# Attention scores made a second time by key, with the maxima carried in rows of the stacked queries

## The reference

```python
q, k, v = (split_heads(x @ W + b) for W, b in ...)     # 16 heads of 16
attn = einsum('bhqd,bhkd->bhqk', q, k) / sqrt(16)
attn = attn + -slopes[:, None, None] * (Tx - 1 - arange(Tx))[None, None, :]
attn = where(causal, attn, finfo.min)
p = softmax(attn, axis=-1)
out = einsum('bhqk,bhkd->bhqd', p, v).transpose(0, 2, 1, 3).reshape(Bx, Tx, C)
return out @ Wo + bo
```

## Time and profile before

| | us |
|---|---|
| runs, median of 3 | 2093.58 (2092.94 to 2094.51) |
| profiled execution | 2089.43 |
| its span, first to last instruction | 2087.6 |
| TensorE busy in the span | 1864.1 (89%) |
| VectorE busy | 1351.8 (65%) |
| ScalarE busy | 928.1 (44%) |
| GpSimd busy | 570.2 (27%) |

### The profile page before, as it was taken

One profiled execution on the slowest core, in us unless ns is written; L12 is line 12 of the kernel. 1 busy time (PEld: TensorE's weight loads), 2 busy tenths in 40 slices (PEclk: granted clock), 3 DMA queues, 4 the chain that ended last, 5 costly groups with the idle time before them and its releaser, 6 DMA issues.

```text
span 2087.6 us, 26257 instructions
## 1 busy us (share of the span) xinstructions
PE 1864.1 (89%) x9448; PEld 1417.8 (68%) x9448; DVE 1351.8 (65%) x1828; ACT 928.1 (44%) x1769; POOL 570.2 (27%) x386
## 2 busy tenths in 40 slices
PE   5699999998779798998777999999999967998898
PEld 2488888887334353544335888888888856777787
DVE  4656656567099999999994566565775444665433
ACT  1223333333466577766442233233333326887322
POOL 1500000002177678677850000000000014545000
PEclk8899999999889999999998999999999987999899
DMA  4263223110022122122214232231230034553100
GB/s 174 66 174 100 76 88 103 62 62 26 21 66 76 56 66 66 62 66 65 67 41 124 67 99 79 86 99 66 61 102 7 1 70 99 102 109 65 31 21 21
DMA packets 86891, 150.86 MB, mean 72 GB/s; under 512 B 14376, under 2 KB 24232, under 8 KB 86248
## 3 DMA queue, kind: packets, MB, share of 16 engines
q1 hardware_dynamic: 86760, 149.17, 24.8%
HBM read 134.84 MB, written 14.29 MB: 71 GB/s over the span
## 4 chain that ended last, share of the span: by engine, by line
PE 69%; DVE 14%; ACT 8%; issue 6%; POOL 1%; DMA 1%; SPq 1%; DVEq 0%; ACTq 0%; POOLq 0%
PE psum L159 18%; PE psum L160 18%; PE psum L161 18%; DVE scan_state L1372 6%; PE psum L1225 4%; PE psum L1138 3%; ACT attn_p L1846 2%; ACT attn_p L1841 2%; PE psum L1165 1%; DVE scan_state L1379 1%; DVE attn_neg_max L1918 1%; PE psum L1146 1%; PE psum L1197 1%; PE psum L276 1%; PE psum L1688 1%
## 5 line engine op out<-in xcount | busy, mean ns | idle before, releaser
L1041 POOL TENSOR_TENSOR scan_state<-scan_delta_u,scan_B_rows 128x1024 f32<-128x1024 f32 x128 | 302.5, 2373 | 166.6 <-PE psum L1225 117.9
L159 PE MATMUL psum<-xnT_hi,moe_w_hi 128*128 128x512 f32 x800 | 317.2, 396 | 3.8 <-DVE moe_w_lo L700 3.8
L160 PE MATMUL psum<-xnT_lo,moe_w_hi 128*128 128x512 f32 x800 | 315.7, 395 | 0.0
L161 PE MATMUL psum<-xnT_hi,moe_w_lo 128*128 128x512 f32 x800 | 313.1, 391 | 0.0
L1372 DVE TENSOR_TENSOR_SCAN scan_state<-psum,scan_state 128x1024 f32<-128x1024 f32 x128 | 292.2, 2283 | 3.1 <-POOL scan_state L1041 2.5
L768 DVE TENSOR_TENSOR moe_gated_up<-moe_gate_rows,psum 128x512 f32<-128x512 f32 x200 | 137.6, 688 | 240.1 <-PE psum L161 152.8
L410 POOL TENSOR_SCALAR rstd<-mean_var 128x2 f32<-128x2 f32 x48 | 10.6, 220 | 1024.0 <-DVE mean_var L444 1023.5
L724 ACT ACTIVATE moe_hidden<-psum 128x512 f32<-128x512 f32 x200 | 119.6, 598 | 378.4 <-PE psum L161 378.4
L1225 PE MATMUL psum<-scan_state,ident 128*128 128x512 f32 x512 | 257.3, 627 | 0.0
L159 PE MATMUL psum<-moe_w_hi,moe_hidden_hi 128*128 128x256 f32 x800 | 227.2, 284 | 11.8 <-DVE moe_hidden_lo L789 10.6
L161 PE MATMUL psum<-moe_w_hi,moe_hidden_lo 128*128 128x256 f32 x800 | 226.9, 284 | 0.0
(11 more groups left out here) (214 smaller groups left out, 3543.1 us busy)
## 6 DMA issues: line engine op xcount, KB each, us to landing
scan_B_rows<-scan_B SPq DMA_DIRECT2D x128, 256.0 KB, 3.1
moe_gate_rows<-gate_table SPq DMA_DIRECT2D x176, 128.0 KB, 2.9
moe_w_raw<-moe_pack SPq DMA_DIRECT2D x50, 384.0 KB, 3.8
attn_stack<-attn_rows SPq DMA_DIRECT2D x96, 128.0 KB, 5.4
moe_gate_rows<-gate_table SPq DMA_DIRECT2D x32, 224.0 KB, 3.0
ffn_w_raw<-ffn_pack SPq DMA_DIRECT2D x16, 384.0 KB, 3.5
moe_gate_rows<-gate_table SPq DMA_DIRECT2D x32, 160.0 KB, 2.7
moe_gate_rows<-gate_table SPq DMA_DIRECT2D x24, 192.0 KB, 2.9
```

Of the source, the lines that this page charges most:

```text
L159: e.matmul(out, wH, xH, start=start, stop=False)
L160: e.matmul(out, wH, xL, start=False, stop=False)
L161: return e.matmul(out, wL, xH, start=False, stop=stop)
L1041: e.tensor_tensor(self.st[q % self.NBUF][:], self.dtu[:, 2 * h:2 * h + 2, :], self.Bs[:, q % self.RING, :].unsqueeze(1).broadcast_to([P, 2 ...
```

## The change

The probabilities are no longer made with queries on partitions and turned. Instead:
- `scores(n)` stays for the maxima alone. Its first mask product moves ahead of the four products of 256 columns. It now waits for the maxima and the shift of the unit before, not for the exponentials.
- The negative maxima (128x8) are turned by one transpose (`turn`), copied as a high and a low part (`shift`, VectorE), sent to DRAM by ScalarE's queue (`send`) and fetched into rows 50 and 51 of the stacked queries (`fetch`); the stacked keys have rows of ones there.
- `shifted(n)` makes the scores a second time with keys on partitions, over 52 rows, so that the maximum is already taken off: three thirds of 512 columns in banks 3 to 5, each with a mask product behind it.
- `exps(n)` is three exponentials of 128x512 straight into the operand of `weigh`. ScalarE's and VectorE's copies are gone, and so are GpSimd's divisions.
- `weigh(n)` makes eight more products, of the same operand with ones, for the sums. For each pair of units VectorE takes the reciprocal of 128x256 sums and multiplies (`out`).
- The jobs are spread anew; both output products come one chunk later (units 1 and 3), the norm's steps in units 2 to 5. The stack loads wait for `shifted` instead of `scores`. Four more DMAs fill constant rows at the start.

```diff
-    JOBS = {(0, 1): ("v1", 0), (1, 1): ("q0", 1), (2, 0): ("ln0", -1), (2, 1): ("k0", 1), (3, 1): ("out1", -1),
-            (4, 1): ("q1", 1), (5, 1): ("k1", 1), (6, 0): ("ln1", -1), (6, 1): ("v0", 1), (7, 1): ("out0", 0)}
+    JOBS = {(0, 1): ("q0", 1), (1, 0): ("out0", -1), (1, 1): ("k0", 1), (2, 1): ("v1", 0), (3, 0): ("out1", -1),
+            (3, 1): ("q1", 1), (4, 1): ("k1", 1), (5, 1): ("ln0", -1), (6, 1): ("ln1", -1), (7, 1): ("v0", 1)}
...
-                e.dma_start(self.st[0][r:r + 2, kb, :, :].bitcast(F32),
-                            self.fixed[0][32:34, :].unsqueeze(1).broadcast_to([2, 4, CHUNK])
-                            ).then_inc(self.s_fill.sem, 16)
+                for st, at in ((self.st[0], r), (self.st[1], r + 2)):
+                    e.dma_start(st[at:at + 2, kb, :, :].bitcast(F32),
+                                self.fixed[0][32:34, :].unsqueeze(1).broadcast_to([2, 4, CHUNK])
+                                ).then_inc(self.s_fill.sem, 16)
...
-                        e.wait_ge(self.s_S.sem, self.s_S.at(8 * (c - 1) + 4 * kb + 4))
+                        e.wait_ge(self.s_S2.sem, self.s_S2.at(3 * (8 * (c - 1) + 4 * kb + 4)))
...
-                e.wait_ge(self.s_exp.sem, self.s_exp.at(n))
+                e.wait_ge(self.s_nm.sem, self.s_nm.at(2 * n))
+                e.wait_ge(self.s_shL.sem, self.s_shL.at(n))
...
+            e.wait_ge(self.s_nm.sem, self.s_nm.at(2 * n + 2))
+            e.transpose(ps[0:8, 0, 0:P], self.nm[:, n % 3, :], k.ident[:]).then_inc(self.s_T.sem, 1)
+
+        def shifted(n):
+
+
+            kb, b, at = place(n)
+            r = slice(at, at + self.ROWS + 2)
+            e.wait_ge(self.s_sent[n % 2].sem, self.s_sent[n % 2].at(16 * (n // 2 + 1)))
+            q, kk = self.st
             for t in range(3):
...
+                if n:
+                    e.wait_ge(self.s_exp.sem, self.s_exp.at(3 * n - 2 + t))
+                for x in range(4) if t == 2 else (2 * t, 2 * t + 1):
+                    keys, at = b * SEQ + P * (t == 2), b * SEQ + P * (t == 2)
+                    w = P if t == 2 else SEQ
+                    col = x * P if t == 2 else x % 2 * SEQ
+                    m = e.matmul(ps[:, 3 + t, col:col + w], kk[r, kb, x, keys:keys + P], q[r, kb, x, at:at + w],
+                                 start=(col == 0), stop=False)
+                heads = 4 if t == 2 else 2
+                m = e.matmul(ps[:, 3 + t, :].rearrange("p (x t) -> p x t", x=heads)[:, :, 0:P], self.one[:],
+                             self.turned[:].unsqueeze(1).broadcast_to([P, heads, P]), start=False, stop=True)
+                m.then_inc(self.s_S2.sem, 1)
...
+                e.wait_ge(self.s_exp.sem, self.s_exp.at(3 * n + t + 2))
+                for what in range(2):
+                    for x in range(4):
+                        mine = slice(half * HD, (half + 2) * HD)
+                        w = self.ones[:, mine] if what else self.v[:, 2 * b + t, 4 * kb + x, mine]
+                        at = 32 * x
+                        if t == 0:
+                            m = e.matmul(ps[at:at + 32, 6, what * SEQ:(what + 1) * SEQ], w,
+                                         self.pt[:, n % 2, x // 2, x % 2 * SEQ:(x % 2 + 1) * SEQ],
+                                         start=(half == 0 and what == 0), stop=False)
...
         scores(0)
+        turn(0)
         scores(1)
+        turn(1)
+        scores(2)
+        e.wait_ge(self.s_v.sem, self.s_v.at(2))
+        shifted(0)
         for n in range(self.N):
             c, u = divmod(n, self.UNITS)
             if n + 2 < self.N:
-                scores(n + 2)
-            job(c, u, 0)
-            turn(n)
+                turn(n + 2)
             if n:
                 weigh(n - 1)
+            job(c, u, 0)
+            if n + 3 < self.N:
+                scores(n + 3)
             job(c, u, 1)
+            if n + 1 < self.N:
+                shifted(n + 1)
         weigh(self.N - 1)
         c = NCH - 1
-        self.vacant(e, ("out1", c))
-        output(c, 1)
+        for p in range(2):
+            self.vacant(e, (f"out{p}", c))
+            output(c, p)
...
+        def exps(n):
+            for t in range(3):
+                e.wait_ge(self.s_S2.sem, self.s_S2.at(3 * n + t + 1))
+                if n > 1 and t == 0:
+                    e.wait_ge(self.s_pv.sem, self.s_pv.at(n - 1))
+                e.activation(self.pt[:, n % 2, t, :], ps[:, 3 + t, :], ACT.Exp).then_inc(self.s_exp.sem, 1)
+
+        def send(n):
+
+            e.wait_ge(self.s_shL.sem, self.s_shL.at(n + 1))
+            e.dma_start(self.shifts[n % 2].rearrange("i j q -> j i q"),
+                        self.sh[:, n % 2, :, :].bitcast(F32)).then_inc(self.s_away[n % 2].sem, 16)
+
+        def fetch(n):
+            c, kb, b, half = self.unit(n)
+            at = 64 * half + self.ROWS
+            e.wait_ge(self.s_away[n % 2].sem, self.s_away[n % 2].at(16 * (n // 2 + 1)))
+            e.dma_start(self.st[0][at:at + 2, kb, :, b * SEQ:(b + 1) * SEQ].bitcast(F32),
+                        self.shifts[n % 2].rearrange("i (x h) q -> i x (h q)", h=2)).then_inc(self.s_sent[n % 2].sem, 16)
...
             if n + 2 < self.N:
-                exps(n + 2, 0)
-            job(c, u, 0)
-            if n + 2 < self.N:
-                exps(n + 2, 1)
+                send(n + 2)
             if n and n % 2 == 0:
                 out_hi(n // 2 - 1)
             job(c, u, 1)
-            keep(n, 0)
-            keep(n, 1)
+            if n + 2 < self.N:
+                fetch(n + 2)
+            if n + 1 < self.N:
+                exps(n + 1)
...
+        def out(m):
+            e.wait_ge(self.s_pv.sem, self.s_pv.at(2 * m + 2))
+            e.reciprocal(self.rec[:, m % 2, :], ps[:, 6, SEQ:]).then_inc(self.s_rec.sem, 1)
+            e.wait_ge(self.s_rec.sem, self.s_rec.at(m + 1))
+            if m > 1:
+                e.wait_ge(self.s_oL.sem, self.s_oL.at(m - 1))
+            e.tensor_tensor(self.o[:, m % 2, :], self.rec[:, m % 2, :], ps[:, 6, 0:SEQ], ALU.mult).then_inc(self.s_o.sem, 1)
...
+        def shift(n):
+            e.wait_ge(self.s_T.sem, self.s_T.at(n + 1))
             if n > 1:
...
+                e.wait_ge(self.s_away[n % 2].sem, self.s_away[n % 2].at(16 * (n // 2)))
+            e.tensor_copy(self.sh[:, n % 2, 0, :], ps[0:8, 0, 0:P]).then_inc(self.s_shH.sem, 1)
+            e.wait_ge(self.s_shH.sem, self.s_shH.at(n + 1))
+            e.tensor_tensor(self.sh[:, n % 2, 1, :], ps[0:8, 0, 0:P], self.sh[:, n % 2, 0, :].bitcast(F32),
+                            ALU.subtract).then_inc(self.s_shL.sem, 1)
...
             if n + 2 < self.N:
-                maxima(n + 2)
+                shift(n + 2)
+            if n and n % 2 == 0:
+                out(n // 2 - 1)
+            elif n > 1:
+                out_lo((n - 1) // 2 - 1)
             norm(c, u)
             job(c, u, 0)
-            if n and n % 2 == 0:
-                out_lo(n // 2 - 1)
+            if n + 3 < self.N:
+                maxima(n + 3)
             job(c, u, 1)
-            keep(n)
+        out(self.N // 2 - 1)
         out_lo(self.N // 2 - 1)
```

166 lines of the change are left out of this document (60 added, 106 removed).

## The result

| | before | after |
|---|---|---|
| median of the runs, us | 2093.55 (2092.94 to 2094.51, 4 runs) | 2147.79 (2145.08 to 2155.3, 4 runs) |
| profiled execution, its span | 2089.43, 2087.6 | 2145.08, 2143.2 |
| ratio | | 1.0268 (95% interval 1.0251 to 1.0284) |

The change costs 54 us. The forecast was 2131 with a range of 2104 to 2157: the direction and the range held, the value was 17 us too low. The profiled executions are 55.65 us apart, where the sum gave 37.6. The busy times of the changed kernel by stretch show the whole stage. The stretches are: first scores to unit 0, then chunk 0, 1, 2, and chunk 3 with the end. The columns are start:end, length, busy time of PE, PEld, DVE, ACT and POOL with counts, granted TensorE clock, DMA share, GB/s.

A forecast was written before the change was run, and what follows sets the result against it. Prediction took TensorE's own issue as the bound after the change, a chunk 61.1 us against 49.6. Its terms summed to +37.6 us on the profiled execution, 2127, median 2131 us; range 2104 to 2157.

The forecast's parts named there:

- fills, to the first scores: Start of the stage: the chain runs over SP's fills, 0.55 us each and more with the gap; four more, +2.0 us.
- first scores to unit 0: Start of the stage: passes ending at 5.1, 10.3 and 13, then scores by key at half clock; 15.8 against 13.85, +1.9 us.
- chunk 0: First chunk: 58.0 us against 53.6, with 1.4 for VectorE in unit 2 and 1.5 for half clock; +4.4 us.
- chunks 1 and 2: Middle chunks: 61.1 us each against 49.6, TensorE issuing at full clock; +23.0 us together.
- chunk 3 and the end: Last chunk to the stage's last addition: 55.9 us against 49.8, with both outputs now there; +6.1 us.
- The products with ones: Weighing on TensorE: they queue behind the products with v, +0.45 and +0.2, taken as 0.64 us a unit.
- The shape changes: TensorE's scores: going between 50-row and 128-row products and back costs 0.33 us; scores 2.03, by key 2.36 us.
- the first two rivals: TensorE: inserted shape changes cost nothing, 2114, chance 0.2; on top, ones products run beside those with v, 2095, chance 0.1.
- the second rival: TensorE: with shape changes free, ones products ride beside those with v, saving 0.64 us a unit: 2095, chance 0.1.
- The reciprocal is hidden: VectorE, even units: reciprocal of 128x256 taken as 2.1 us; VectorE just fits in TensorE's unit, so nothing queued behind costs time.
- VectorE would be next: VectorE's maxima end at 6.3 us, or 7.4 in units 2 and 4; were TensorE faster, VectorE would bound.
- the third rival: Maxima's DMA round trip: sends and fetches behind a stack load land in 5.4 instead of 2.6 us; +14 to +28, 2152, chance 0.2.

The follow-up runs named there:

- the old mask place: Changed kernel with the three masks of the scores by key put together and the scores' first mask back behind the 256-column products: 2111.28 us, ratio 1.0100.
- the added products: Changed kernel with six more 512-column products in four last-chunk units, with 128 or 32 columns of weights: ratios 1.0277 and 1.0262.
- the full-size added products: Changed kernel with six more products of 128 rows by 512 columns, 128 columns of weights, in four last-chunk units: 2143.8 us, ratio 1.0277.

## Why the prediction came out as it did

By the terms of its sum, against the profiled executions:

| term | predicted | measured |
|---|---|---|
| up to the last addition of the stage before | 0 | +4.08 |
| fills, to the first scores | +2.0 | +2.01 |
| first scores to unit 0 | +1.9 | +6.16 |
| chunk 0 | +4.4 | +7.88 |
| chunks 1 and 2 | +23.0 | +24.44 |
| chunk 3 and the end | +6.1 | +11.68 |
| cast, and all behind the stage | +0.2 | -0.60 |
| sum | +37.6 | +55.65 |

**Right, and shown.** That TensorE becomes the bound: 61.80 us busy of 61.80, no wait. The products with ones at 0.64 us a unit: 1.43 us for the weighing, to the hundredth, and 0.429 us for the first four by themselves. The shape changes: the pair at 0.33 measured 0.34 to 0.39, and the first two rivals (2114 and 2095) fall with them. (Where the prediction says that the sum without the shape changes is the second rival, it is the first, 2114.) The reciprocal is hidden: shown by leaving it out. That VectorE would be next if TensorE were faster came true too, in units 2, 4 and 6 with the old mask place. I had taken 2.1 us for it against the slope of the earlier trace rows, which gives 1.77; it took 1.76, so the slope was the better guide. Fills +2.0 against +2.01. The scores came out at 2.03 as predicted; the turn took 0.20 for 0.15 and the scores by key 2.41 for 2.36, and these 0.1 us a unit are most of the 1.4 us by which chunks 1 and 2 exceed their term.

**The step that failed** is a size: TensorE's clock. The sum allows for the half clock only in the start, and there with times that are too short for it, and with 1.5 us in chunk 0. Three of the terms are short by 4.3, 3.5 and 5.6 us. In the start each pass of scores, maxima, turn and shift takes 6.15 us at half clock, where 5.1 and 5.2 had been put. The third scores take 3.61 us for 2.7, and the scores by key, said to be at half clock but put at 2.8, take 4.10 (2.41 at full clock). In the last chunk the granted clock is 0.86; the added products show 6.6 to 7.0 us for it. The kernel before has 0.90 there as well, so a part was in the baseline, and I hadn't looked. Chunk 0 is of the same kind, and it lies in two units:

```profile
1748.03:1757.71 9.68, 8.90 (x30) 6.07 (x29) 3.22 (x5) 2.49 (x4) 0.00 (x0) 0.63 0.01 2
1772.02:1781.15 9.13, 9.12 (x61) 5.99 (x62) 4.26 (x8) 2.09 (x4) 0.00 (x0) 0.81 1.00 156
```

Unit 0 is 3.6 us longer than the prediction's prices give it at the full clock (5.97 - 1.43 + 1.50 = 6.04), and 0.78 us of it is a wait for VectorE. Unit 3 has no wait and takes 7.56 us at a clock of 1.00 in the kernel with the full-size added products, which has the same code there: 1.6 us more. Against that stand the 1.5 us allowed, and unit 2, where VectorE's work showed with less than the 1.4 us put.

**Luck in the range.** The measured 2147.8 lies outside 2122 to 2145, where the prediction had put half of its chances. It lies in the band of the third rival, and the range holds it only because half of that band was taken in. The mechanism of that rival wasn't what made the time.

**The late round trip**, the third rival at 2152, came nearest to the value and for the wrong reason. In the changed kernel's profiled execution TensorE waits for the shift rows 0.4 us in all. It does meet them, with the same order of work, for up to 1.61 us in other executions, and where TensorE got faster for 3.06 and 2.12 us.

**Not the change.** +4.08 us stand ahead of the stage. The ten other profiled kernels with a form of the changed stage, whose code is the same up to there, reach the last addition of the stage before at 1695.97 to 1704.26 us, the kernel before at 1700.31, the changed one at 1704.39. The executions differ by that much, and the first stages aren't touched. The median of the changed kernel is 54.2 us above that of the kernel before all the same, and its other three runs have no trace; why they aren't faster by that 4 us stays open, though in other kernels the same code of that chunk took 58.7 to 71.2 us.

## What to carry to other kernels

Count the changes between row shapes on TensorE as you count its products: here 0.34 to 0.39 us for every out and back, so products of one shape belong together, masks last. Before work is put together, look at what it covered: the turn lost 1.2 us a unit when its cover moved. And read the granted clock of the thin stretches of the kernel before (its first and its last chunk) before a sum is made at the full clock; a wait that can be split, as that for the exponentials, gave most in such stretches here. Last, a bound is one of several: after three pairs of shape changes were gone, VectorE held three units in eight.

## What the hardware showed beyond this

TensorE's clock falls without a wait in the records: 0.57 in a stretch that is busy from end to end, and 0.99 in the same stretch with 24 more products, wide or narrow. A start that was kept at the full clock for 10 us lost it within the first wait for VectorE. And VectorE's reciprocal on PSUM goes by its slope, 1.76 us for 256 elements in each partition.
